# A decoder layer on one core: the 24 pairs of sequences run in a mixed order instead of layer by layer

## The reference

```
x = x + self_attention(norm(x))            # causal; q = k = v = norm(x), no weights
x = x + cross_attention(norm(x), ctx, bias)# q from x, k and v from ctx; scores = q k + bias[b, h]
                                           # bias is 16 x 16 x 128 x 128: 1 MB for each sequence
x = x + ffn_block(norm(x))                 # norm, plain attention with weights and a residual,
                                           # norm, a gate picks 1 of 8 experts per row (argmax),
                                           # relu(h w1 + b1) w2 + b2 of that expert, a residual
```

## Time and profile before

| what | value |
|---|---|
| median of the runs | 433.36 us |
| span of the profiled execution, first to last instruction | 431.3 us |
| PE busy | 313.1 us (73%) |
| POOL busy | 254.1 us (59%) |
| DVE busy | 249.6 us (58%) |
| ACT busy | 198.4 us (46%) |
| mean granted clock of TensorE | 0.906 of full speed |

### The profile page before, as it was taken

The page is one execution under the profiler, slowest core; times in us unless marked ns, Lnnn a source line. Parts: engine busy times, 40 slices in busy tenths (PEclk is TensorE's granted clock), DMA queues, the critical chain, the costliest instruction groups (busy, mean ns, idle before and its releaser), DMA issues.

```text
span 431.3 us, 9910 instructions
## 1 busy us (share of the span) xinstructions
PE 313.1 (73%) x3435; PEld 203.1 (47%) x3435; DVE 249.6 (58%) x592; ACT 198.4 (46%) x390; POOL 254.1 (59%) x365
## 2 busy tenths in 40 slices
PE   1376888776779999989778788898875500199994
PEld 0133333432456666666544444444443400099893
DVE  5135454458999999997356455665622250067773
ACT  3347555544455565565344536456464200045451
POOL 5853343315889898999996638736340327324454
PEclk9969888999999999999899989999997555589998
DMA  6101443210358977921125990000000002323330
GB/s 165 31 2 56 123 117 110 74 38 14 97 156 184 219 191 162 212 27 22 12 26 136 283 297 24 2 2 2 2 2 2 1 24 108 95 53 103 93 90 18
DMA packets 67040, 36.36 MB, mean 84 GB/s; under 512 B 36253, under 2 KB 56864, under 8 KB 66992
## 3 DMA queue, kind: packets, MB, share of 16 engines
q1 hardware_dynamic: 57040, 15.79, 17.4%
q10 hardware_dynamic: 8448, 16.78, 13.7%
q0 software_dynamic: 1504, 3.16, 2.1%
HBM read 28.48 MB, written 7.69 MB: 84 GB/s over the span
## 4 chain that ended last, share of the span: by engine, by line
PE 43%; issue 16%; POOL 15%; DVE 13%; ACT 8%; DVEq 1%; DMA 1%; POOLq 0%; ACTq 0%; SPq 0%
PE pair_banks L562 23%; PE work_bank L562 9%; POOL biased L413 4%; DVE biased L1019 4%; ACT xn L847 4%; POOL routed_rows L545 3%; PE pair_banks L565 3%; PE work_bank L565 3%; PE small_bank L565 3%; PE small_bank L562 2%; POOL rstd L380 2%; DVE rowmax L1034 1%; ACT outT L886 1%; DVE att L1065 1%; POOL q_lane L390 1%
## 5 line engine op out<-in xcount | busy, mean ns | idle before, releaser
L880 ACT ACTIVATE probs<-pair_banks 128x1024 f32<-128x1024 f32 x96 | 97.5, 1023 | 68.6 <-PE pair_banks L565 36.0
L413 POOL TENSOR_TENSOR biased<-biased,rowmax 128x1024 f32<-128x1024 f32 x32 | 60.5, 1899 | 15.7 <-DVE rowmax L1026 15.5
L562 PE MATMUL work_bank<-probs,vaug 128*32 128x128 f32 x1536 | 53.6, 282 | 5.5 <-ACT hn2T L894 3.4
L562 PEld LDWEIGHTS work_bank<-probs,vaug 128*32 128x32 f32 x1536 | 40.3, 112 | 15.7 <-issue 8.6
L1041 DVE TENSOR_TENSOR pair_banks<-pair_banks,causal 128x1024 f32<-128x1024 f32 x16 | 19.7, 1233 | 47.7 <-PE pair_banks L562 47.7
L1034 DVE TENSOR_REDUCE rowmax<-pair_banks 128x8 f32<-128x1024 f32 x32 | 38.9, 1215 | 13.5 <-PE pair_banks L562 13.5
L374 POOL TENSOR_SCALAR vareps<-meanvar 128x2 f32<-128x2 f32 x32 | 7.4, 233 | 62.6 <-DVE meanvar L995 61.5
L562 PE MATMUL pair_banks<-q_lane,kT 32*128 32x512 f32 x256 | 42.3, 734 | 1.7 <-DVE biased L1019 1.7
L1019 DVE TENSOR_TENSOR biased<-pair_banks,bias_in 128x1024 f32<-128x1024 f32 x32 | 38.8, 1214 | 7.3 <-PE pair_banks L562 3.8
L552 POOL DMA_INDIRECT out<-vaug x23 | 22.6, 984 | 33.1 <-DVE vaug L1230 20.3
L562 PE MATMUL pair_banks<-k_lane,qT 32*128 32x512 f32 x256 | 37.5, 654 | 5.9 <-DVE biased L1019 4.0
(11 more groups left out here) (143 smaller groups left out, 581.0 us busy)
## 6 DMA issues: line engine op xcount, KB each, us to landing
bias_in<-in_w SPq DMA_DIRECT2D x16, 256.0 KB, 7.3
routed_rows<-filler SPq DMA_DIRECT2D x2, 1028.0 KB, 9.1
vaug<-routed_rows SPq DMA_DIRECT2D x23, 64.5 KB
biased<-routed_rows SPq DMA_DIRECT2D x23, 64.0 KB
ctx_in<-in_ctx SPq DMA_DIRECT2D x8, 128.0 KB, 4.1
att_scratch<-att SPq DMA_DIRECT2D x16, 64.0 KB, 5.4
att_rows<-att_scratch SPq DMA_DIRECT2D x16, 64.0 KB, 2.9
routed_rows<-filler SPq DMA_DIRECT2D x1, 899.5 KB, 12.0
```

The costliest lines, as they stand in the source:

```text
L413: nc.gpsimd.tensor_tensor(v, v, rowmax[:, b % 2, 8 * half:8 * half + 8].unsqueeze(2).to_broadcast([128, 8, S]), ALU.subtract).then_inc(s_s ...
L562: return nc.tensor.matmul(o, lhsT, rhs, start=start, stop=stop, **kw)
L880: nc.scalar.activation(probs[:, b % 2, 2 * half:2 * half + 2, :], pair("exp", b, half), ACT.Exp, scale=1.0 if layer(b) == CROSS else SCALE ...
```

## The change

A string gives the order of the 24 pairs, and tables made from it replace the arithmetic on slot numbers:

```
-FIRST_CROSS, FIRST_FFN = B, 2 * B
-CROSS_PAIR, FFN_PAIR = B // 2, B
-BIAS_AT = {4: 16, 6: 17, 8: 18, 10: 19, 12: 20}
+ORDER = "SSSSSCCSCSCSCCFCCFFFFFFF"
+PLAYER = ["SCF".index(p) for p in ORDER]
+NUMBER = [ORDER[:q].count(p) for q, p in enumerate(ORDER)]
+WIDE = [q - ORDER[:q].count("S") for q in range(NP)]
+BIAS_AT = {1: 0, 2: 1, 4: 2, 6: 3, 8: 4}
+EXPERTS_AT = 33
 def layer(b):
-    return b // B
+    return PLAYER[b // 2] if b < NB else FFN
+def batch(b):
+    return 2 * NUMBER[b // 2] + b % 2
+def wide(b):
+    return 2 * WIDE[b // 2] + b % 2
+def slot_of_pair(kind, n):
+    return [q for q in range(NP) if PLAYER[q] == kind][n]
+def projections(b):
+    c = [b - 4] if 0 <= b - 4 < NB and layer(b - 4) == CROSS else []
+    return c + ([b - 3] if 0 <= b - 3 < NB and layer(b - 3) == FFN else [])
+def has_maxes(b):
+    return b < NB and layer(b) != SELF
 def pair_turns():
-        if FIRST_CROSS <= b + 2 < NB:
+        if has_maxes(b + 2):
...
 # PE, each slot
-                if FIRST_CROSS <= b + 2 < NB:
+                if has_maxes(b + 2):
                     score_maxes(b + 2)
-                if b < FIRST_CROSS:
+                if layer(b) == SELF:
                     self_scores(b)
...
-                elif b < FIRST_FFN:
+                elif layer(b) == CROSS:
                     cross_scores(b, 0)
                     out_transposed(b - 2)
                     cross_scores(b, 1)
...
 # DVE, each slot
-                maxes = FIRST_CROSS <= b + 2 < NB
+                maxes = has_maxes(b + 2)
...
-                if b < FIRST_CROSS:
+                if layer(b) == SELF:
                     mask_second_half(b)
+                if b == 1:
+                    dve.wait_ge(s_w, WEIGHTS)
+                    nc.vector.tensor_scalar(cols[:, 0:1], cols[:, 0:1], SCALE, None, ALU.mult).then_inc(s_wq, 1)
+                    nc.vector.tensor_scalar(wx["xq"][:], wx["xq"][:], SCALE, None, ALU.mult).then_inc(s_wq, 1)
-                if b == 8:
+                if b == 6:
                     dve.wait_ge(s_dve_const, 5)
...
 # POOL, each slot
+                if b == 3:
+                    pool.wait_ge(s_w, WEIGHTS)
-                if b == 8:
-                    pool.wait_ge(s_w, WEIGHTS)
 # SP, each slot
-                if FIRST_CROSS <= b - 3 < FIRST_FFN:
+                if b >= 3 and layer(b - 3) == CROSS:
                     read_attention(b - 3)
-                if b > FIRST_FFN:
+                if b >= EXPERTS_AT:
                     load_expert(b)
```

More of the change, by code:

```diff
@@ L62, in pair_turns, with rowmax_before @@
     return {turn: n % 3 for n, turn in enumerate(turns)}
+def rowmax_before(b):
+    before = [c for c in range(b % 2, b, 2) if layer(c) != SELF]
+    return before[-1] if before else None
 PAIR_BANKS = pair_turns()
@@ L747, in _ @@
                         add_outputs(b - 1)
-                    if values:
-                        v_products(q + 2)
-                elif b < FIRST_FFN:
+                    if ahead:
+                        max_transposed(b + 1)
+                    if values is not None:
+                        v_products(values)
+                elif layer(b) == CROSS:
                     cross_scores(b, 0)
@@ L753, in _ @@
                     cross_scores(b, 1)
-                    if values:
-                        v_products(q + 2)
+                    if values is not None and player(values) == CROSS:
+                        v_products(values)
                     add_outputs(b - 1)
-                    if b + 1 == FIRST_FFN:
+                    if ahead:
                         max_transposed(b + 1)
+                    if values is not None and player(values) == FFN:
+                        v_products(values)
                 else:
@@ L763, in _ @@
                         add_outputs(b - 1)
-                    if b + 1 < NB:
+                    if ahead:
                         max_transposed(b + 1)
@@ L767, in _ @@
                         ffn_scores(b)
-                    if values:
-                        v_products(q + 2)
-                    if c is not None:
+                    if values is not None:
+                        v_products(values)
+                    for c in ready[:1]:
                         attention_transposed(c)
@@ L773, in _ @@
                         less_maxes(b)
-                if c is not None and b < FIRST_FFN:
-                    attention_transposed(c)
-                if b % 2 == 1 and CROSS_PAIR <= q + 3 < NP:
+                if layer(b) != FFN:
+                    for c in ready[:1]:
+                        attention_transposed(c)
+                if b % 2 == 1 and q + 3 < NP and player(q + 3) != SELF:
                     qk_products(q + 3)
@@ L911, in _ @@
             for b in range(LAST_SLOT):
-                q, c = b // 2, projected_first(b)
-                if b < FIRST_FFN:
+                q, ready = b // 2, projections(b)
+                ffn = layer(b) == FFN
+                if not ffn:
                     exponentials(b, 0)
@@ L916, in _ @@
                     load_bias(BIAS_AT[b])
-                elif FIRST_CROSS <= b and b + NBIAS < FIRST_FFN:
-                    load_bias(b + NBIAS)
-                if b < FIRST_FFN:
+                elif layer(b) == CROSS and batch(b) + NBIAS < B:
+                    load_bias(batch(b) + NBIAS)
+                if not ffn:
                     exponentials(b, 1)
-                    if b % 2 == 0:
+                    if b % 2 == 0 and q + 3 < NP:
                         normalise(q + 3)
@@ L924, in _ @@
                     take_out(b - 1)
-                if c is not None:
+                for c in ready[:1]:
                     take_attT(c)
-                if FIRST_FFN <= b and b % 2 == 0 and q + 3 < NP:
+                if ffn and b % 2 == 0 and q + 3 < NP:
                     normalise(q + 3)
@@ L939, in _ @@
                         take_hT(q + 3)
-                if FIRST_FFN <= b < NB:
+                if ffn and b < NB:
                     exponentials(b, 1)
-                if projected_second(b) is not None:
-                    take_attT(projected_second(b))
+                for c in ready[1:]:
+                    take_attT(c)
                 if b in LAST_NORMS:
@@ L1094, in _ @@
                 q = b // 2
-                maxes = FIRST_CROSS <= b + 2 < NB
-                for c in (projected_first(b - 1), projected_second(b - 1)):
-                    if c is not None:
-                        residual(c)
+                maxes = has_maxes(b + 2)
+                values = q + 2 if b % 2 == 0 and q + 2 < NP and player(q + 2) != SELF else None
+                for c in projections(b - 1):
+                    residual(c)
                 if b == 0:
@@ L1125, in _ @@
                                             ALU.mult).then_inc(s_dve_const, 1)
-                if FIRST_FFN <= b + 1 < NB:
+                if b + 1 < NB and layer(b + 1) == FFN:
                     take_maxT(b + 1)
```

256 lines of the change are left out of this document (133 added, 123 removed).

## The result

The changed kernel takes 453.38 us (median; 451.14 to 455.18) against 432.69 us, the median of four runs of the kernel before (433.36 was that of three): a ratio of 1.0471, 95% interval 1.0427 to 1.0514. It is slower by 20.7 us, where 450 (+16.6) was forecast. In this document medians hold all executions, while ratios and intervals leave out those more than 1.5% above the fastest of their kernel, so the two can differ by some tenths of a per cent. The profiled execution has a span of 450.3 us, 19.0 more than before.

The account below looks back on a forecast made before the run. S pairs were taken as chains of waits, C pairs as filling PE, DVE and POOL; at seams DVE and PE take turns. 12.9 + 1.6 + 1.3 + 0.5 = 16.3 on 431.3 gives 447.6, plus 2.1: 450 us, range 442 to 458.

Parts of the forecast that it names:

- S pairs with C maxima: S pairs 7, 9 and 11, each making the maxima of the C pair behind it: 17.1 us each.
- S and C pair together: S pairs 7, 9, 11 with C pairs 6, 8, 10: 81.5 us after, 68.6 before, so +12.9.
- Pairs 5 and 6: First C pair follows as before; pair 6, with no older C attention to project yet, estimated at 8.6 us.
- Pair 12: C pair before a C pair; POOL also spreads the F pair's queries: 13.4 us (12.8 to 14.5).
- the place that I had left at 0 with an end of 2.7: Self adds in full C slots 24 and 25, possibly stretched where DVE and POOL meet: 0, upper end 2.7 us.
- Pairs 13 and 14: C pair set by PE, 13.2 us (12.5 to 14); F pair near POOL's limit, 13.8 (13 to 15.5).
- Start: The first five S pairs follow each other as before, at 10.05 us each, so no difference there.
- Projections and SP: Double projection in slot 31, +1.3 us (0 to 2); C outputs of slots 32, 33 behind slot 34's filler, +0.5.
- 1 and 2 (overlap): PE's waits in S pairs get filled: all of them, 429.3 us, 12%; half of them, 440 us, 9%.
- 4 (the seam from C to F pays it back): Gains at the C-to-F seam return what S pairs lose; needs 16 of 37.8 us: 433.5 us, 5%.
- 3, the lower clock: TensorE drops to its lower clock in the new S pairs, 10.3 us more: 460 us, 10%.
- one of my own signs of being wrong: Score products at 2 us in S slots would show the forecast wrong.

Follow-up runs that it names:

- mix_swap: Changed kernel, but in S slots making C maxima PE makes self scores before the next score products and DVE masks before the bias add: 439.64 us.
- mix_fill: Changed kernel plus seven extra, overwritten matmuls on PE in the even S slots without maxima, while PE waits for ACT: 449.96 us, ratio 1.0417.
- mix_pemask: Changed kernel, but PE adds the causal mask to both halves of self scores, where DVE added it to the second: 443.68 us, ratio 1.0207.
- mix_early: Changed kernel, but at each C-to-S seam the S slot's first score product moves up into the C slot ahead: 453.98 us, ratio 1.0527.
- two_s: Changed kernel with order SSSSSCCSCSSCCCCCFFFFFFFF: two seams from C to S instead of three, no F pair among C: 446.34 us, ratio 1.0318.
- f_only: Changed kernel with order SSSSSSSSCCCCCCCFCFFFFFFF: S and C by layer, one F pair ahead of the last C pair: 436.02 us, ratio 1.0035.
- layered: Changed kernel with only the order put back to SSSSSSSSCCCCCCCCFFFFFFFF, the rest of the change kept: 433.99 us, ratio 1.0049.
- lay_fill: layered plus seven extra, overwritten matmuls in the even S slots 0 to 12 while PE waits for ACT: 428.06 us, ratio 0.9934.

## Why the prediction was right

The direction, the mechanism and most of the size held; that the total came so near is in part luck, since terms of the sum were off both ways. Step by step:

- *S pairs with C maxima*: 17.1 forecast for pair 11, 16.74 measured. *S and C pair together*: 27.4 and 28.4 forecast for pairs 7, 8 and 9, 10; 27.17 and 27.94 measured. Pairs 5 and 6: 14.6 + 8.6 = 23.2 forecast, 22.46 measured. Cut where PE's list of the S pair ends (120.33 and 147.84), pairs 7 and 9 took 16.7 and 17.1, and pairs 8 and 10 took 10.5 and 10.9 with PE's wait at their start. That DVE and PE take turns is shown by the traces (idle times on both sides) and by mix_swap, which takes one of the turns away; the straight line over none to three seams shows that the cost goes with the seams. But the terms were built on rows at a clock of 1.00, and these pairs had 0.94 and 0.88. At 1.00 pairs 7 and 8 took 26.21 (mix_fill), 1.2 under the forecast; the clock made up for it.
- *Pair 12* was the step that was mis-sized: 13.4 forecast, 16.90 measured. I built it on the 12.82 of a C pair among C pairs, though the row of the pair behind an S pair, 14.60, stood beside it. The other 2.3 are mostly the clock, 0.90 here with a score product at 2.09 (183.77). mix_pemask has the same instructions in this pair, the same waits for F's values and a stretched self add too, and at 1.00 it took 15.04:

```profile
168.70:183.74 15.04, 12.21 (x134) 8.58 (x134) 12.96 (x22) 7.50 (x16) 14.68 (x15) 1.00 0.52 143
```

  A self add of this pair was stretched from 0.29 to 1.21:

```profile
188.17 1.21 DVE L1120 TENSOR_TENSOR x_sb<-x_sb,att 128x128 f32<-128x128 f32 x1
```

```profile
187.34 1.90 POOL L442 TENSOR_TENSOR biased<-biased,rowmax 128x1024 f32<-128x1024 f32 x1
```

  The add began while POOL subtracted and ended with it (189.4 and 189.2). This is the place that I had left at 0 with an end of 2.7; it took 0.9 there. The Trainium skill's rule (SBUF — State Buffer, Who interferes with whom) agrees with this add, and with the three other long ones of this trace (85.66, 128.41 and 155.72), which also end just behind a POOL instruction that had begun before them. The pair's other add took 0.29 (178.50): POOL's subtraction began only at 179.93, so the rule asks for no wait there. The median of 292 ns was no ground for 0: it comes from the adds in the self stage. The only two that stood among C's work in the kernel before were both long:

```profile
111.77 1.65 DVE L1070 TENSOR_TENSOR x_sb<-x_sb,att 128x128 f32<-128x128 f32 x1
...
119.16 1.22 DVE L1070 TENSOR_TENSOR x_sb<-x_sb,att 128x128 f32<-128x128 f32 x1
```

- *Pairs 13 and 14*: 13.2 and 13.8 forecast, 13.22 and 14.91 measured; pair 14 had a clock of 0.89 and took 13.84 at 1.00 in mix_fill.
- *Start.* By these terms slot 8 was to begin its score product at 91.31 - 3 x 10.05 = 61.2; it began at 63.74, after a mean clock of 0.89. Runs with the same instructions up to there began it at 61.71 (mix_early, 0.92) and 62.03 (two_s, 0.94), so most of this is TensorE's clock, which falls at other places in each execution.
- *Projections and SP*, +1.8, do not show in the sum: slots 30 to 41 took 86.23, the same work before (slots 28 to 39, two C and four F pairs) 86.44 (187.44 to 273.88). But the double projection is there: slot 31 took 8.60 (228.66 to 237.26), as much as slot 35 before.

```profile
228.66 1.14 PE L591 MATMUL pair_banks<-k_lane,qT 32*128 32x512 f32 x8
...
237.26 1.14 PE L591 MATMUL pair_banks<-k_lane,qT 32*128 32x512 f32 x8
```

  So the C pair with slot 31 took 16.77 for 13.24 before, and a gain that the sum had at nothing hid it: the last C pair took 14.63 (237.26 to 251.89) and 17.39 before (200.68 to 218.07), where PE waited 2.62 and score products took 2.00, and the four F pairs took 1.0 less. SP's term was 0: PE waited for no DMA in slots 36 and 37.

The sum of pairs 4 to 14 is 156.75 for 153.9 (+2.85), the start +2.6, and all behind pair 14 -2.7, of which 1.8 are the terms for projections and SP, which came to nothing in the sum: 19.0 for 16.3. The last stretch, from the last score product to the end, took 121.4 to 125.8 in the traces of this document, so the 0.9 that is left is within scatter.

*Rivals.* 1 and 2 (overlap) fell: PE and DVE ran in turn. 4 (the seam from C to F pays it back) fell with the result, and f_only gained nothing that can be told; the 2.8 us gained on the last C pair are far from the 16 it needed. 3, the lower clock, is true in part, and one of my own signs of being wrong came true with it: score products at 2 us stand in S slots (111.60, 138.62). The clock cost 1.0 in pairs 7 and 8, 1.9 in pair 12 and 1.1 in pair 14, each against a trace that had 1.00 there (for pair 12 that of mix_pemask, whose S slots differ), and about 2 by slot 8; for pairs 9 and 10 no trace with the same instructions had 1.00. It is not the main cause: at 1.00 the first seam still cost 26.21 where 22.9 was paid. Nor is it the way of C's attention through DRAM: of the waits that show, PE's only one for it in the attention part is 0.79 us (109.43).

## What to carry to other kernels

In this kernel work for an idle engine would have helped only if the engines' in-order lists had let it run beside the others; where a buffer is passed to and fro between two engines, adding work to one lengthens the turn of both. Before an order is changed, find the seam in the trace that the new order repeats, price it with the pair behind it, and count how often it will occur. A wait that a bank makes can be cheaper to remove by the order of two instructions on one engine than by the order of the layers.

## What the runs showed of the hardware that was not expected

Matmuls whose result nobody reads made the kernel faster. In the self stage of layered TensorE waits 2.15 us in each of five pairs in a row, and the self scores behind it often ran at 2.09 us (63.91, 74.19), at other times at 1.14 (54.87); the mean granted clock over 20 to 85 us was 0.89. Seven matmuls (1.7 us) in that wait kept the granted clock at 1.00 over 20 to 85 us, that is at the 2.4 GHz level throughout, and lay_fill took 5.0 us less than layered by the ratios, 0.7 a pair. Its trace is 8.0 us ahead by slot 14 (83.18 against 91.20) and 5.9 at the end; the stretch behind the last score product, which varies from trace to trace, took 125.8 in it and 122.1 in layered.
